# Scores and exponentials of the first four attention heads moved in between the query products of a fused graph-network kernel

## What is computed

```
h = relu(layernorm(x));  x = x + relational_layer(h)      # 3 relations, 3 node types
h = relu(layernorm(x))
qkv = h @ W_qkv.T + b_qkv                                 # 8 heads of 64
scores = sum(Q[receivers] * K[senders]) * 64**-0.5        # one per edge and head
smax = segment_max(scores); ex = exp(scores - smax[receivers])
att = ex / segment_sum(ex)
x = x + segment_sum(att * V[senders]) @ W_ff.T + b_ff
```

## Time and profile before

| | us |
|---|---|
| median of 3 timed runs | 316.27 (316.02 to 317.65) |
| profiled execution, its own time | 315.79 |
| its span in the trace | 314.0 |
| TensorE products busy | 290.9 (93%) |
| VectorE busy | 199.1 (63%) |
| ScalarE busy | 143.8 (46%) |
| GpSimd busy | 71.4 (23%) |
| chain that ended last: share on TensorE | 79% |

### The profile page before, as it was taken

The page is one execution under the profiler, slowest core; times in us unless marked ns, Lnnn a source line. Parts: engine busy times, 40 slices in busy tenths (PEclk is TensorE's granted clock), DMA queues, the critical chain, the costliest instruction groups (busy, mean ns, idle before and its releaser), DMA issues.

```text
span 314.0 us, 5396 instructions
## 1 busy us (share of the span) xinstructions
PE 290.9 (93%) x1966; PEld 227.1 (72%) x1966; DVE 199.1 (63%) x481; ACT 143.8 (46%) x282; POOL 71.4 (23%) x98
## 2 busy tenths in 40 slices
PE   2848799999999999999899999999799999999995
PEld 1513244544677788678787889999699998999984
DVE  5899977996133344334457942884987758576742
ACT  1151344432325422524434442677877666665731
POOL 7038004210483234620002410420001102020202
PEclk9999999999999999999999999999999999999999
DMA  5672697111162400042500000000000100000001
GB/s 184 230 238 83 242 370 274 61 41 38 38 229 76 134 3 3 2 134 78 191 0 0 2 0 3 0 0 3 0 2 0 37 2 0 37 0 35 3 33 32
DMA packets 10970, 22.29 MB, mean 71 GB/s; under 512 B 950, under 2 KB 966, under 8 KB 10938
## 3 DMA queue, kind: packets, MB, share of 16 engines
q1 hardware_dynamic: 8772, 16.80, 15.8%
q10 hardware_dynamic: 1366, 2.45, 2.3%
q0 software_dynamic: 800, 2.62, 2.2%
HBM read 15.60 MB, written 6.26 MB: 70 GB/s over the span
## 4 chain that ended last, share of the span: by engine, by line
PE 79%; DVE 12%; ACT 3%; DMA 2%; issue 2%; DVEq 0%
PE banks L1260 14%; PE banks L1206 9%; PE banks L1246 9%; PE banks L1151 8%; PE banks L1348 7%; PE banks L1332 7%; PE banks L1104 6%; PE banks L1321 6%; PE banks L1370 4%; DVE key_hot L835 3%; DVE row_hot L842 2%; DMA raw<-in_L_gnn_W_qkv_dram 2%; PE banks L1236 1%; PE banks L1193 1%; PE banks L1360 1%
## 5 line engine op out<-in xcount | busy, mean ns | idle before, releaser
L1104 PE MATMUL banks<-key_hot,row_hot 128*128 128x480 f16 x120 | 33.1, 426 | 8.5 <-DVE key_hot L835 8.5
L1018 DVE CUSTOM_DVE_ANT_0 s_sb<-banks,mask_add 128x640 f32<-128x640 f32 x40 | 32.6, 821 | 13.1 <-PE banks L1321 13.0
L675 ACT ACTIVATE p_sb<-s_sb,neg_max 128x640 f32<-128x640 f32 x40 | 32.9, 824 | 12.5 <-DVE neg_max L1018 12.2
L835 DVE TENSOR_SCALAR key_hot<-iota,picked 128x480 f16<-128x480 f16 x120 | 36.8, 373 | 0.0
L1206 PE MATMUL banks<-adjT,h 128*128 128x320 f16 x240 | 33.1, 299 | 0.4 <-DVE zT_even L894 0.4
L1104 PEld LDWEIGHTS banks<-key_hot,row_hot 128*128 128x128 f16 x120 | 12.8, 107 | 26.3 <-DVE key_hot L835 9.2
L1206 PEld LDWEIGHTS banks<-adjT,h 128*128 128x128 f16 x240 | 23.3, 98 | 9.8 <-DVE zT_even L894 0.7
L1332 PE MATMUL banks<-ident,p_sb 128*128 128x128 f32 x200 | 29.8, 275 | 0.3 <-ACT pT L682 0.2
L1260 PE MATMUL banks<-w_hl,zT_even 128*128 128x512 f32 x120 | 29.3, 394 | 0.0
L505 POOL TENSOR_TENSOR msgT<-msg_f,msgT 128x128 fp32r<-128x128 f32 x20 | 8.6, 461 | 90.3 <-ACT msgT L696 90.3
L1321 PE MATMUL banks<-k_hi,q_st 128*128 128x320 f32 x80 | 26.8, 343 | 2.0 <-DVE neg_max L1018 2.0
(11 more groups left out here) (179 smaller groups left out, 473.6 us busy)
## 6 DMA issues: line engine op xcount, KB each, us to landing
w_self<-in_L_gnn_W_self_dram SPq DMA_DIRECT2D x3, 1024.0 KB, 10.5
raw<-in_L_gnn_W_rel_dram SPq DMA_DIRECT2D x3, 1024.0 KB, 14.7
raw<-in_L_gnn_W_qkv_dram SPq DMA_DIRECT2D x3, 1024.0 KB, 5.2
sorted_rows<-zero_rows ACTq DMA_DIRECT2D x1, 1792.0 KB, 11.6
self_rows<-hs SPq DMA_DIRECT2D x7, 256.0 KB, 2.2
hs<-sorted_rows SPq DMA_DIRECT2D x1, 1280.0 KB, 7.2
xs<-in_x_dram SPq DMA_DIRECT2D x1, 1024.0 KB
raw<-in_L_gnn_W_ff_dram SPq DMA_DIRECT2D x1, 1024.0 KB, 5.2
```

The source lines that it names most:

```text
L675: nc.scalar.activation(p_sb[:, n % NPR, :], s_sb[:, n % NS, :], ACT.Exp, scale=-1.0, bias=neg_max[:, it, h:h + 1], accum_out=denom[:, it, ...
L835: return nc.vector.tensor_scalar(to_key, iota[:], float(KEYS * w), key, ALU.add, ALU.is_equal)
L1018: nc.vector.tensor_tensor_reduce(s_sb[:, n % NS, :].rearrange("p (a j) -> p a j", a=2), banks[:, c:c + 2, 0:HALF], mask_add[:, it, :].rear ...
L1104: mm(banks[:, w % 2, 0:KEYS], row_hot[:, w % 2, k, :], key_hot[:, w % 2, k, :], start=(k == 0), stop=True, skip_group_check=True).then_inc ...
```

## The change

The queue order: after the query units of pair 1 the common schedule gets the item `("scores", 0)`, after those of pair 2 `("scores", 1)`. At these items each engine runs the steps of the attention list with places from 0 to below 2, and from 2 to below 3.2. What remains runs after the units, as before. The last pair is split in the unit loop like the others, and minimum 2 waits for the split of pair 2, since its buffer lies where that pair's `qk_f` was.

The buffers: `s_sb`, `p_sb`, `msg_f`, `r_sb`, `msgT` and `norm_hl` lay over the whole of the transposed query, key and value weights (`wqkvT`). These are still being read while the first scores run, so `s_sb` moves beside `qk_f`, and the `p_sb` buffers into the key columns, which are no longer needed. Shapes stay as they are. The step functions on each engine are gathered in a local `attend(kind, n)`; its text is that of the loop before.

```
-        s_sb = place("s_sb", o_r4, [P, NS, NP], F32)
-        p_sb = place("p_sb", o_r4 + 7680, [P, NPR, NP], F32)
+        qk_f = [place(f"qk_f{i}", o_ss + 2560 * (1 - i), [P, NP], F32) for i in range(2)]
+        s_sb = [place(f"s_sb{i}", o_ss + 2560 * (3, 2, 1)[i], [P, NP], F32) for i in range(NS)]
+        p_sb = [place(f"p_sb{i}", o_r4 + 2048 + 6144 * i, [P, NP], F32) for i in range(NPR)]
...
-        schedule += [("q", a, half) for a in range(KD) for half in range(2)]
-        ring = [u for u in schedule if u[0] not in ("gemm", "sum", "ln")]
+        for a in range(KD):
+            schedule += [("q", a, 0), ("q", a, 1)]
+            if a in (1, 2):
+                schedule.append(("scores", a - 1))
+        ring = [u for u in schedule if u[0] not in ("gemm", "sum", "ln", "scores")]
...
-        attention = [(kind, n) for _, kind, n in sorted(placed, key=lambda step: step[0])]
+        placed = sorted(placed, key=lambda step: step[0])
+        attention = [[(kind, n) for at, kind, n in placed if a <= at < b] for a, b in ((0, 2), (2, TURN), (TURN, 1e9))]
...
             for u in schedule:
+                if u[0] == "scores":
+                    for step in attention[u[1]]:
+                        attend(*step)
+                    continue
...
-            for step in attention:
+            for step in attention[2]:
+                attend(*step)
...
-                    if u[2] == 1 and u[1] < KD - 1:
+                    if u[2] == 1:
                         split_q(u[1])
...
+                    if n == NS - 1:
+                        dve.wait_ge(s_qk, split_count(2 * KD - 1))
                     if n >= NS:
                         dve.wait_ge(s_exp, n - NS + 1)
...
-                    if n == 1:
-                        split_q(KD - 1)
```

More of the change, by code:

```diff
@@ L595, in unit_part @@
                         act.wait_ge(s_qk, split_count(n - 1))
-                    ins = nc.scalar.activation(qk_f[:, n % 2, half * HALF:(half + 1) * HALF], bank(u)[:, 0:HALF],
+                    ins = nc.scalar.activation(qk_f[n % 2][:, half * HALF:(half + 1) * HALF], bank(u)[:, 0:HALF],
                                                ACT.Identity, bias=bqk[:, n:n + 1],
@@ L664, in _ @@
                         me = 64 * hh
-                        nc.scalar.activation(q_st[me:me + 64, 2 * a + hh, :], qk_f[me:me + 64, (KD + a) % 2, :],
+                        nc.scalar.activation(q_st[me:me + 64, 2 * a + hh, :], qk_f[(KD + a) % 2][me:me + 64, :],
                                              ACT.Copy).then_inc(s_qhi, 1)
-            for step in attention:
[L669 to L696, removed]
+            for step in attention[2]:
+                attend(*step)
         @block.vector
@@ L925, in split_q @@
             def split_q(a):
-                f = qk_f[:, (KD + a) % 2, :]
+                f = qk_f[(KD + a) % 2][:, :]
                 for hh in range(2):
@@ L934, in split_k @@
             def split_k(a):
-                f = qk_f[:, a % 2, :]
+                f = qk_f[a % 2][:, :]
                 for hh in range(2):
@@ L988, in _, with attend @@
             all_groups()
[L990 to L1010, removed]
+            def attend(kind, n):
                 if kind == "smax":
@@ L1061, in _ @@
                                             ).then_inc(s_fin, 1)
+            for u in schedule:
+                if u[0] == "scores":
+                    for step in attention[u[1]]:
+                        attend(*step)
+                    continue
+                if u[0] == "sum":
+                    it = u[1]
+                    dve.wait_ge(s_self, 16 * NT)
+                    dve.wait_ge(s_acc, it + 1)
+                    chain(nc.vector.tensor_tensor(self_sum[:, it, :], banks[:, it, :], self_sum[:, it, :],
+                                                  ALU.add))
+                    chain(nc.vector.scalar_tensor_tensor(out=xs[:, it, :], in0=self_sum[:, it, :], scalar=0.0,
+                                                         in1=xs[:, it, :], op0=ALU.max, op1=ALU.add))
+                    statistics(1, it).then_inc(s_var, 1)
+                elif u[0] == "ln":
+                    it = u[1]
+                    dve.wait_ge(s_std, 2 + it)
+                    factors(1, it, it + 1)
+                elif u[0] != "gemm":
+                    unit_part(u)
+            for step in attention[2]:
+                attend(*step)
         @block.tensor
@@ L1332, in _ @@
                         ins = nc.tensor.transpose(banks[:, 5 + n % 2, i * P:(i + 1) * P],
[L1333 removed]
+                                                  p_sb[h % NPR][:, jt * P:(jt + 1) * P], ident[:])
                     ins.then_inc(s_tr, 1)
@@ L1374, in _ @@
                         ins.then_inc(s_ff, 1)
+            for u in schedule:
+                if u[0] == "scores":
+                    for step in attention[u[1]]:
+                        attend(*step)
+                    continue
+                if u[0] in ("sum", "ln"):
+                    continue
+                if u[0] != "gemm":
+                    unit(u)
+                    continue
+                _, r, it = u
+                if it == 0:
+                    pe.wait_ge(s_wlo, KD * (r + 1))
+                    pe.wait_ge(s_ufree, number[("z", r, KD - 1, 1)] + 1)
+                if r == 0:
+                    if it == 0:
+                        pe.wait_ge(s_blo, 1)
+                    mm(banks[:, it, :], cnt6[:, it * P:(it + 1) * P], bhl[:], start=True, stop=False,
+                       skip_group_check=True)
+                ins = gemm(banks[:, it, :], zT[r % 2], it, w_hl[r % 2], 0, D, start=False)
+                if r == R - 1:
+                    ins.then_inc(s_acc, 1)
+                elif it == NT - 1:
+                    ins.then_inc(s_gemm, 1)
+            for step in attention[2]:
+                attend(*step)
 def load_bounds(eng, nc, bounds, row, nw, last):
```

40 lines of the change are left out of this document (33 added, 7 removed).

## The result

| | before | changed |
|---|---|---|
| median of 13 timed runs, us | 316.05 (315.79 to 317.65) | 317.60 (317.19 to 320.05) |
| ratio of the changed to before | | 1.0048 (95%: 1.0032 to 1.0064) |
| profiled execution, us; span | 315.79; 314.0 | 317.78; 316.0 |
| TensorE products busy, us | 290.9 | 291.6 |
| granted clock of the profiled execution | 1.00 | 0.995 |

What follows compares the result with a forecast made beforehand. TensorE was taken as the bound, with nothing after the ramp to absorb losses. Queue waits of +1.1 us on the profiled 315.79 gave 316.9 us; on the median 316.27 the forecast was 317.4 us, range 315.2 to 318.5.

Steps and rivals of the forecast that it cites:

- Bound: TensorE bounds the kernel, busy 68.00 of 68.00 us from 232 to 300, so nothing later absorbs what the ramp loses.
- Buffer places at 0, no table load: New buffer places, and ScalarE alternating exponentials with copies without loading tables, were each costed at 0.
- ScalarE's and VectorE's queues: In the ramp, query copies wait behind exponentials, minima behind splits; last query copy done at 223.39, TensorE idle 2.5 us.
- Turn 3 and the shift: On TensorE in the ramp, turn 3 comes at 227.46 instead of 226.35 us, a shift of +1.1 us that stays.
- queue term: Ramp loss from query copies held behind exponentials that wait for VectorE: +1.1 us, allowed 0.7 to 1.6.
- The number: Whole kernel: 316.9 us for the profiled execution, 317.4 us on the median of the timed runs.
- The clock rival: TensorE's clock falls after standing still 2.5 us in the ramp, costing 1.9 us more: 319.3 us, chance 0.08.
- the prediction's own last sign: Prediction is wrong if turns behind TensorE's long ramp wait take clearly more than 0.62 us for four.
- The cover works: Query copies don't stand behind exponentials, so at most all 2.29 us of TensorE's ramp idle goes: 314.0 us, chance 0.12.
- recovered: Some of the 1.1 us comes back between turn 3 and the first value products: 316.3 us, chance 0.12.
- What would show it: Ramp signs: turn 0 near 223.6 us after 2 to 3 us idle, first value products near 232.5 instead of 231.4.

Runs made afterwards that it cites:

- places only: Changed kernel with only its new buffer places, every engine in the order of the kernel before: 316.00 us against 316.31, ratio 0.9993.
- changed again: The changed kernel itself, unaltered, timed again on another chip beside the kernel before: 317.53 us against 315.95, ratio 1.0049.
- first pair only: Changed kernel, but only scores, minima and exponentials 0 and 1 moved, behind the query units of pair 1: 316.83 us against 316.33 before, ratio 1.0025.
- first pair later: Changed kernel, but only scores, minima and exponentials 0 and 1 moved, behind the query units of pair 2: 320.56 us against 316.33 before, ratio 1.0124.
- exponentials later: Changed kernel with ScalarE's moved exponentials one pair later, TensorE and VectorE in the changed order: 315.82 us against 316.31 before, ratio 0.9983.
- all three ordered: Changed kernel with the ramp order of ScalarE, VectorE and TensorE written out by when inputs come: 314.86 us against 316.33 before, ratio 0.9956.
- more delay: Changed kernel with two unused copies added on ScalarE ahead of the query copies of pair 3: 318.97 us against 316.31 before, ratio 1.0092.
- two queues ordered: Changed kernel with the ramp order of ScalarE and VectorE written out, TensorE's left as changed: 315.62 us against 316.33 before, ratio 0.9980.

## Why the prediction was right, point by point

- *Bound.* Right: from 233 to 301 us of the changed kernel TensorE is busy 68.00 of 68.00, as in the earlier trace rows, and whatever the ramp lost reached the end.
- *Buffer places at 0, no table load.* Right: places only gave 0.9993, and the changed kernel has the same four table loads as before, none behind the first exponential. What the Trainium skill says (ScalarE: Activation LUTs, "Table sets: the hidden batching unit"), that cheap functions lie in every set, agrees with that. The prediction read its advice as one against alternating copies and exponentials; it is to batch calls by set and not by function, so it doesn't speak against this change.
- *ScalarE's and VectorE's queues.* Right to within 0.2 us. With 0.47 us taken off: exponential 0 at 215.66 (215.66 forecast), copies of pair 2 at 217.31 (217.31), exponential 2 at 221.74 (221.62), last copy done at 223.49 (223.39), turn 0 at 223.76 (223.6), the gap 2.39 (2.5).
- *Turn 3 and the shift.* Forecast 227.46 and +1.1 us. Without a fall +1.21 (changed again), so the queue term was 0.1 short. With a fall turn 3 stands at 227.85 and the shift is 1.52.
- *The number.* The forecast of 317.4 us came closer to 317.60 than its working did to the shift. The shift of the medians was 1.55 us and not 1.1; the forecast started from the median of three runs, 316.27, which 13 runs put at 316.05, and this makes up for half of what the shift lacked. That it counts as no change by the 0.5% bound, at 1.0048, was luck as much as working.
- *The clock rival.* This is the step that was mis-sized. I gave it 0.08 as a case of its own, with 1.9 us on top. A mean clock of 0.995 or less is there in 12 of 18 executions, and the fall costs 0.3 us in the one that the first profile shows. By the prediction's own last sign (the turns behind the long wait take clearly more than 0.62 us for four) it was wrong on this point: turns 1 and 2 took 1.91 us for eight at 225.55, while in changed again, without a fall, they took 0.60 and 0.63. Two misreadings: I took a fall as rare after dense work, since the 1.34 us of the earlier trace rows did no harm, and I priced it as if TensorE had been the bound all through the low stretch. Where it is, the price is as large as I thought: 1.5 us in first pair only (40.87 against 39.38) and 2.2 in first pair later.
- *The cover works, recovered.* Neither happened. Something like the first came about only when the orders were rewritten: exponentials later, then all three ordered, gave -0.5 and -1.5 us.
- *What would show it.* Turn 0 released by the bank of the last query copy, minimum 0 right behind a split, no idle in the product stage: all seen. The first value products near 232.5: 232.58 in changed again (its offset off), but 232.89 in the first profile, for the clock.

## What to carry to other kernels

A step moved forward on several engines with one common item lands in each queue in front of whatever that engine did next; on the engine that is late, it blocks work whose input is ready. Before moving, lay out all the queues by hand with durations from the trace, and put each step on each engine where its input comes. And price a new gap on TensorE twice, once as idle time, and once as a possible fall of its clock behind it, which costs what the waits in that stretch don't cover.

## What the runs showed of the hardware that I had not expected

- A gap of 2.39 us on TensorE, behind 90 us with 88.55 us of products (132 to 222), was followed by a fall to the lower level in the first profile and by none in changed again. One of 3.43 us in more delay was followed by none either. A mean clock of 0.995 or less was there in 12 of 18 executions of the changed kernel. The kernel before, whose longest gap in the ramp is 1.34 us, had a mean clock of 0.995 or less in 9 of 60 executions of the three later comparisons, at 317.1 to 317.9 us instead of near 316.1. Exponentials later (gaps 0.83 and 1.19) had it in none of 12, all three ordered (0.66) in none of 6, two queues ordered (0.99) in two of 9, places only in one of 12. In the mean clock alone the place of a fall can't be seen: the profile of first pair later has one between 36 and 42 us besides that in the ramp, so some of these may lie in the early stages too.
- That early fall bears out how the prediction told the level by durations. In it the count products take 607 ns (median of six from 37.6 us on), in the kernel before at the same place 376.
- A fall can come after a gap or in it. In the changed kernel turn 0 started at 224.23 at full speed, and the clock fell at about 224.9. In first pair later it fell at about 225.4, inside the gap of 2.59 us and 2 us behind the one of 0.91.
- Products that nobody needs made the ramp of a kernel 2.2 us shorter (42.53 to 40.35), by keeping the clock up. The medians differ by more (4.2 and 1.4 us above the kernel before), but part of that can lie in early falls.
